# Attention in a macaron block: softmax division by packed rows in place of TensorE transposes

## The chip, the cores and the metric

The kernel runs on one core of a Trainium2 chip. The metric is the device time of one execution in microseconds, as the median of several runs. TensorE multiplies matrices into eight PSUM banks of 128 x 512 f32; VectorE, ScalarE and GpSimd (POOL) work elementwise; SyncE (SP) issues nearly all DMAs, in program order.

## The reference, cut to what matters

```python
def attn(x, Wq, Wk, Wv, Wo):              # x: (16, 256, 256), 16 heads of 16
    q, k, v = split_heads(x @ Wq.T), split_heads(x @ Wk.T), split_heads(x @ Wv.T)
    q, k = rope(q), rope(k)
    scores = einsum('bhqd,bhkd->bhqk', q, k) / 4
    scores = where(causal, scores, -inf)
    out = einsum('bhqk,bhkd->bhqd', softmax(scores), v)
    return merge_heads(out) @ Wo.T

x = x + 0.5 * ffn(layernorm(x))           # 256 -> 1024 -> 256, ternary weights, exact gelu
x = x + attn(layernorm(x))
x = x + 0.5 * ffn(layernorm(x))           # same weights
```

## The kernel before

The program has three stages that share the residual `res` in SBUF: a feed-forward stage over 8 chunks of 512 rows, attention over 16 batches of 256 rows, and the feed-forward stage again (FFN2 here). f32 products are made as sums of products of a high and a low part (fp32r, or three bf16 parts for q and k).

Attention is a software pipeline written out by hand. `periods` steps p from -2 to 16; p = 1 to 10 are a hardware loop of five turns with two periods each. Each period has two steps, h = 0 and 1, of eight heads. Every engine has its own `step(p, h)`, and in period p it works on several batches: the loads of batch p+2, the maxima (scores S, with the queries on partitions) of batch p+1, the transposed scores T, exponentials and products with v (PV) of batch p, Q/K/V and rope of batch p+3, layer norm and its transposes XT of batch p+4, and the output product of batch p-1. `p.has(n)` is true where batch p+n exists.

A step has six units of S and six of T on TensorE, alternating. S goes to a ring of three banks (`s_ring`), from which VectorE takes row maxima (`maxima`, L863). The maxima, negated by rows of minus ones, enter T as three more rows of the contraction, so that T is ready for the exponential (ScalarE, L985, from a ring of two banks). A `fence` (L1060) puts the causal mask and a large negative constant into a bank ahead of the products (L1065), as a matmul of the identity with a mask tile. After the units come, in h = 0, OT(p, 0) and QK, in h = 1 ANT, V, OT(p, 1), XT and WO; then MT (transposes of the split maxima, L1141) and PV (L1121, L1124).

PV writes the heads transposed: `o_bank` holds for two groups of four heads, each at partitions 32 j, sixteen rows of numerators and one row of softmax sums, because `v_pad` has v in columns 0 to 15 and a one in column 16 (zeros up to 31). To divide, ScalarE copies the bank to `o_sb` (`copy_heads`, L977). TensorE transposes it back into `o_bank` in four transposes (`OT`, L1134), so that the sum of a row stands beside its numerators. VectorE takes reciprocals and multiplies (`normed_heads`, L899 and L903) into `att`, and PV of the next half waits for that (`normed`). Once both halves are in, four transposes (`ANT`, L1184) turn `att` once more into `mixed[0]`, ScalarE and VectorE split it into `att_t` (`copy_att` L990, `low_att` L909), and `WO` (L1196) multiplies it with Wo into `mixed[1]`, which `add_output` (L921) adds to the residual. `mixed[0]` is also the bank of Q and of XT, `mixed[1]` that of K and V.

SyncE's step is: `load` of q and k of batch p+2 (waits until T of period p has read those rows); in h = 1 the stores of batch p+3, six DMAs, which wait for POOL's `low`; then `max_rows`, the DMA of the maxima of batch p+1.

At the end (p = 15 and 16) FFN2's first hidden products are put between the units (`hidden_ahead`), and its first y products wait for the last output to be in the residual (`wo_done`).

## Time and profile before

| | us |
|---|---|
| median of 3 runs | 603.77 |
| lowest, highest run | 602.36, 604.93 |
| span of the profiled execution | 600.8 |
| TensorE busy (matmuls) | 567.2, 94% |
| VectorE busy | 458.9, 76% |
| ScalarE busy | 345.2, 57% |
| POOL busy | 229.3, 38% |

The span runs from the first instruction to the last of one profiled execution; what lies around it in a run's own time is not in it, so the 603.77 and the 600.8 are about 3 us apart. The profiled execution has no run time of its own beside its span. A busy share is a mean over all three stages.

### The profile page before, as it was taken

To read this page: it belongs to the slowest core of one execution; us is meant where nothing else is said; L and a number is where in the kernel's file an instruction comes from. 1 tells how busy PE (TensorE), PEld (TensorE's weight loads), DVE (VectorE), ACT (ScalarE), POOL (GpSimd) and SP (SyncE) were. 2 spreads that over 40 slices of the span, in tenths; PEclk is the share of its full clock that TensorE was granted. 3 is DMA by queue.
4 is the path that set the end of the run, shared out by engine and by line. 5 is a ranking of instruction groups with operands and counts; after the bars stand their busy time and mean duration, and the time that the engine had idled before them with its cause. 6 is when DMAs were issued, how large, how long until landed. Compare 5 with 4: busy or idle time off the path is not lost.

```text
span 600.8 us, 17866 instructions
## 1 busy us (share of the span) xinstructions
PE 567.2 (94%) x6596; PEld 496.4 (83%) x6596; DVE 458.9 (76%) x928; ACT 345.2 (57%) x610; POOL 229.3 (38%) x446
## 2 busy tenths in 40 slices
PE   1999999999789999999999999999888999999998
PEld 1789999999668888888888888888665788999997
DVE  5977777779797978879788788877562777777765
ACT  2765454546246666776667766567545655455453
POOL 6383333332665354444544445434141033333310
PEclk9999999999999999999999999999989999999999
DMA  6530000000987567654576546765400011111111
GB/s 221 199 112 6 0 0 0 0 0 1 257 219 207 167 164 208 172 157 146 166 204 177 158 139 175 197 186 159 138 2 3 1 36 35 35 35 35 35 35 36
DMA packets 71190, 63.45 MB, mean 106 GB/s; under 512 B 4178, under 2 KB 64370, under 8 KB 71154
## 3 DMA queue, kind: packets, MB, share of 16 engines
q1 hardware_dynamic: 69970, 62.81, 36.1%
q8 instruction: 25, 0.41, 0.3%
q10 hardware_dynamic: 1184, 0.14, 0.2%
q14 instruction: 11, 0.09, 0.1%
HBM read 33.03 MB, written 29.36 MB: 104 GB/s over the span
## 4 chain that ended last, share of the span: by engine, by line
PE 82%; DVE 10%; DMA 3%; ACT 2%; issue 1%; POOL 1%; SPq 1%; ACTq 0%; DVEq 0%
PE bank L173 18%; PE bank L537 18%; PE bank L1065 13%; PE bank L673 6%; PE bank L1060 6%; PE bank L1121 5%; PE bank L1196 4%; PE bank L1161 3%; PE bank L156 2%; PE bank L1124 2%; PE bank L1134 2%; DVE mx L863 2%; DVE g_lo L257 2%; PE bank L1184 1%; DMA w1f<-w1t 1%
## 5 line engine op out<-in xcount | busy, mean ns | idle before, releaser
L863 DVE TENSOR_REDUCE mx<-bank 128x2 f32<-128x512 f32 (+1 forms) x192 | 118.7, 684 | 31.3 <-PE bank L1065 31.2
L240 ACT ACTIVATE g<-bank,b1c 128x512 f32<-128x512 f32 x128 | 88.0, 690 | 65.6 <-PE bank L173 62.5
L537 PE MATMUL bank<-w2q,g_hi 128*128 128x256 f32 x512 | 124.4, 284 | 1.3 <-DVE g_lo L257 0.9
L537 PE MATMUL bank<-w2q,g_lo 128*128 128x256 f32 x512 | 122.5, 280 | 0.0
L985 ACT ACTIVATE probs<-bank 128x512 f32<-128x512 f32 x192 | 111.2, 597 | 11.9 <-PE bank L1065 4.4
L537 PEld LDWEIGHTS bank<-w2q,g_hi 128*128 128x128 f32 x512 | 96.5, 188 | 2.9 <-DVE w2q L375 1.1
L537 PEld LDWEIGHTS bank<-w2q,g_lo 128*128 128x128 f32 x512 | 96.5, 188 | 0.6
L315 POOL TENSOR_TENSOR res<-res,b2h 128x1024 f32 (+1 forms) x16 | 38.3, 2394 | 133.0 <-DVE xn L147 128.9
L257 DVE TENSOR_TENSOR g_lo<-g,g_hi 128x512 fp32r<-128x512 f32 x128 | 82.8, 689 | 3.1
L173 PE MATMUL bank<-xt_hi,w1q 128*128 128x512 f32 x240 | 77.3, 404 | 2.0 <-DVE xt_lo L167 2.0
L173 PE MATMUL bank<-xt_lo,w1q 128*128 128x512 f32 x240 | 76.4, 400 | 0.0
L1065 PE MATMUL bank<-k,q 99*64 99x128 bf16 (+1 forms) x1024 | 74.4, 246 | 0.0
L1065 PE MATMUL bank<-q,k 102*64 102x256 bf16 (+1 forms) x1024 | 74.3, 246 | 0.0
L173 PEld LDWEIGHTS bank<-xt_lo,w1q 128*128 128x128 f32 x240 | 46.0, 192 | 11.0
L173 PEld LDWEIGHTS bank<-xt_hi,w1q 128*128 128x128 f32 x240 | 44.4, 192 | 12.1 <-issue 3.0
L1060 PE MATMUL bank<-mask_qk,ident_b 128*64 128x128 bf16 (+1 forms) x384 | 47.4, 243 | 4.5 <-DMA k<-qk_slots 1.8
L1060 PE MATMUL bank<-mask_kq,ident_b 128*64 128x128 bf16 (+1 forms) x384 | 48.1, 247 | 1.1 <-ACT probs L985 1.0
L805 POOL TENSOR_TENSOR rot<-by_cos,by_sin 128x512 f32<-128x512 f32 x30 | 38.3, 1280 | 24.1 <-DVE by_sin L683 23.1
L248 DVE CAST g_hi<-g 128x512 fp32r<-128x512 f32 x60 | 25.6, 427 | 28.4 <-ACT g L240 26.9
L162 ACT CAST xt_hi<-bank 128x512 fp32r<-128x512 f32 x32 | 17.3, 590 | 51.3 <-PE bank L156 51.3
L1019 ACT COPY mt<-bank 24x256 bf16<-24x256 bf16 x32 | 11.6, 361 | 58.3 <-PE bank L1141 57.7
L792 POOL TENSOR_TENSOR m_parts<-mx,zero 128x16 bf16<-128x16 f32 x32 | 8.3, 258 | 95.4 <-DVE mx L863 95.4
(129 smaller groups left out, 1170.1 us busy)
## 6 DMA issues: line engine op xcount, KB each, us to landing
qk_slots<-parts SPq DMA_DIRECT2D x32, 384.0 KB, 3.6
q<-qk_slots SPq DMA_DIRECT2D x32, 384.0 KB, 4.0
k<-qk_slots SPq DMA_DIRECT2D x32, 384.0 KB, 4.5
qk_slots<-parts SPq DMA_DIRECT2D x32, 256.0 KB, 3.4
res<-x SPq DMA_DIRECT2D x8, 512.0 KB, 3.6
qk_slots<-parts SPq DMA_DIRECT2D x32, 128.0 KB, 3.2
out<-res SPq DMA_DIRECT2D x7, 512.0 KB, 2.9
w1f<-w1t SPq DMA_DIRECT2D x2, 512.0 KB, 6.1
```

What stands on the lines that cost most here:

```text
L173: last = nc.tensor.matmul(to[:], w1q[:, k, f * P:(f + 1) * P], part[:, k, :], start=i == 0, stop=i == 2 * KC - 1)
L240: nc.scalar.activation(g[:, f, :], of[:], ACT.Gelu, bias=b1c[:, f:f + 1]).then_inc(g_ready, 1)
L257: nc.vector.tensor_tensor(g_lo[:, f, :], g[:, f, :], g_hi[:, f, :].bitcast(F32), ALU.subtract)\
L315: pool.tensor_tensor(res[:, bass.ts(c, CT), :], res[:, bass.ts(c, CT), :], b2h[:].unsqueeze(1).broadcast_to([P, CT, D]), ALU.add).then_inc ...
L537: last = nc.tensor.matmul(to[:, 0:D], part[:, f, t * P:(t + 1) * P], w2q[:, f, :], start=f == 0 and part is g_hi, stop=f == FC - 1 and par ...
L673: last = nc.tensor.matmul(to[:, e * SEQ:(e + 1) * SEQ], w[i][:, k, (2 * t + e) * P:(2 * t + e + 1) * P], x[a][:, k, :], start=n == 0, stop ...
L805: pool.tensor_tensor(rot[:, t, :], by_cos[:, t, :], by_sin[:, t, :], ALU.add).then_inc(rot_s, 1)
L863: nc.vector.tensor_reduce(o, i, AX.X, ALU.max).then_inc(s_done, 1)
L985: nc.scalar.activation(probs[g % 2][:, 512 * u:512 * u + 512], t_ring[n % 2][:], ACT.Exp, scale=0.25)\
L1060: nc.tensor.matmul(to[c, :, c], ident_b[:, c], mask[:, :, c], start=True, stop=False, skip_group_check=True)
L1065: last = nc.tensor.matmul(to[c, :], weights[:, c], moving, start=False, stop=stop, skip_group_check=True)
L1121: nc.tensor.matmul(o[32 * j:32 * j + 32, :], v_pad[par][:, 0, HALF * h + 4 * g + j, :], probs[g][:, j * SEQ:(j + 1) * SEQ], start=True, st ...
```

## The change

The division no longer goes through TensorE. `pad_cols` is all ones, so columns 16 to 31 of `v_pad` all hold ones and the sums stand in rows 16 to 31 of each group. After `copy_heads`, SyncE's new `heads(p, h)` issues five DMAs: one takes the four rows of sums of `o_sb` into `den`, spread over 128 partitions with 16 values each, and four take the numerator rows to their places in `att`, which is now transposed (rows are head and feature, columns are group and query). After both halves VectorE takes one reciprocal of all sums (`reciprocals`). `reciprocal_rows` writes the result to DRAM (`rden_dram`), waits for it and reads it back with every sum repeated for its sixteen rows (`rden_rows`). `normed_heads` is then one product of 128 x 512, from which `copy_att` and `low_att` make `att_t` without a transpose. The rows of Wo are permuted on the host to match. PV waits only for `copy_heads`.

The order is changed with it: `normed_heads` comes first in step h = 1 on VectorE, `low_att` after three of the six maxima, `copy_att` on ScalarE after three of the six exponentials. `hidden_ahead` of chunk part 2 comes later, the output of batch 14 (period 15) is put into period 16, and the output of batch 15 (period 16) into FFN2: its product is taken on VectorE inside chunk 0, its output product is issued on TensorE after chunk 0 into bank 5, and added after chunk 0.

The masks are stored once and repeated by a stride of 0 in `fence`. Some small constants now lie in the memory of `by_cos`; `rope_products` first waits for the constant rows' DMAs.

```diff
@@ -57,6 +57,7 @@
 
 
         scratch = nc.dram_tensor("qk_slots", (BATCH, 2, SLOTS, 2, HD // 2, HEADS, SEQ), BF16, kind="Internal").ap()
+        rden_dram = nc.dram_tensor("rden_slots", (BATCH, 2, 4 * KC * SEQ), F32, kind="Internal").ap()
...
-        mask_qk = sb("mask_qk", [P, 4, P], BF16)
-        mask_kq = sb("mask_kq", [P, 4, P], BF16)
+        mask_qk = sb("mask_qk", [P, P], BF16)
+        mask_kq = sb("mask_kq", [P, P], BF16)
         ones_mean = sb("ones_mean", [P, P])
-        minus_rows = sb("minus_rows", [PARTS, SEQ], BF16)
-        fence_q, fence_k = sb("fence_q", [FENCE, SEQ], BF16), sb("fence_k", [FENCE, SEQ], BF16)
+        att_t = [sb(f"att_t{n}", [P, KC, SEQ], F32R) for n in ("_hi", "_lo")]
...
+        few = by_cos[0:PARTS, 0, :].bitcast(BF16)
+        fence_q, fence_k, minus_rows = (few[:, i * SEQ:(i + 1) * SEQ] for i in range(3))
+        rows_in = [sem(f"att_rows_in{p}") for p in range(2)]
         parts = [sb(f"parts{p}", [P, 2, PARTS, 2 * SEQ], BF16) for p in range(2)]
+        den, rden = (sb(n, [P, 2, KC * SEQ * 4 // P]) for n in ("den", "rden"))
...
+                                            (mask_qk, 0.0), (mask_kq, 0.0), (pad_cols, 1.0),
...
                         dve.wait_ge(xb_ready, gc + 1)
+                        if opening:
+                            of_last.normed_heads(dve)
                         for t in range(CT):
                             if t == 2 and following is not None and not closing:
                                 if before:
                                     split_xt(dve, n, last_hi, last_lo)
                                 else:
                                     split_xt(dve, n)
+                                if opening:
+                                    of_last.low_att(dve)
...
                         chunk(0, 1, 2, BEGUN)
+                        of_last.add_output(dve)
...
                         chunk(0, True, begun=BEGUN)
+                        of_last.copy_att(act)
...
+                            if phase == 1 and into[f] is banks[5]:
+                                pe.wait_ge(wo_done, BATCH + 1)
...
-                            pe.wait_ge(wo_done, BATCH + 1)
+                            pe.wait_ge(wo_done, BATCH)
...
+                        of_last.output(pe)
...
+        def closes(p, n):
+            return p.known and p.p + n == BATCH - 1
+
+        def o_sb(p, n):
+            return by_cos[:, 0, :] if closes(p, n) else o_all[:]
+
+        def att(p, n):
+            return rot[:, 0, :] if closes(p, n) else att_all[:]
+
+        def rden_rows(p, n):
+            return rot[:, 1, :] if closes(p, n) else rden_all[:]
...
+        def normed_heads(dve, p):
+            dve.wait_ge(heads_in, 128 * p.p)
+            dve.wait_ge(rden_in, 16 * p.p)
+            o = att(p, -1)
+            nc.vector.tensor_tensor(o, o, rden_rows(p, -1), ALU.mult).then_inc(normed, 1)
+
+        def copy_att(act, p):
+            act.wait_ge(normed, p.p)
+            nc.scalar.copy(att_t[0][:].rearrange("p k s -> p (k s)"), att(p, -1)).then_inc(att_hi_s, 1)
+
+        def low_att(dve, p):
+            dve.wait_ge(att_hi_s, p.p)
+            nc.vector.tensor_tensor(att_t[1][:].rearrange("p k s -> p (k s)"), att(p, -1),
+                                    att_t[0][:].rearrange("p k s -> p (k s)").bitcast(F32), ALU.subtract).then_inc(att_lo_s, 1)
+
+        def output(pe, p, to=mixed[1]):
+            pe.wait_ge(att_lo_s, p.p)
+            if p.has(3):
+                pe.wait_ge(v_done, p.p + 4)
+            elif p.has(-2):
+                pe.wait_ge(wo_done, p.p)
+            for t in range(QT):
+                for n, (w, a, k) in enumerate(PASSES):
+                    last = nc.tensor.matmul(to[:, t * D:(t + 1) * D], att_t[a][:, k, t * P:(t + 1) * P], wo[w][:, k, :],
+                                            start=n == 0, stop=n == len(PASSES) - 1)
+            last.then_inc(wo_ready, 1)
+
+        def add_output(dve, p, of=mixed[1]):
+            b = p.p - 1
+            dve.wait_ge(wo_ready, b + 1)
+            nc.vector.tensor_tensor(res[:, bass.ts(b, QT), :], of[:].rearrange("p (t d) -> p t d", t=QT),
+                                    res[:, bass.ts(b, QT), :], ALU.add).then_inc(wo_done, 1)
...
+            def heads(p, h):
+                n, half = -1 if h == 0 else 0, (h + 1) % 2
+                sp.wait_ge(o_copied, 2 * p.p + h)
+                if half == 0 and p.has(-1) and not closes(p, n):
+                    sp.wait_ge(att_lo_s, p.p)
+                if half == 0 and p.has(-1) and closes(p, n):
+                    sp.wait_ge(den_s, p.p)
+                of, to = o_sb(p, n), att(p, n)
+                sp.dma_start(den[:, half, :], of[HD:P:32, :]).then_inc(den_in, 16)
+                for j in range(4):
+                    row = (4 * half + j) * HD
+                    sp.dma_start(to[row:row + HD, :], of[32 * j:32 * j + HD, :]).then_inc(heads_in, 16)
+
+            def reciprocal_rows(p):
+                sp.wait_ge(den_s, p.p)
+                sp.dma_start(rden_dram[p.p - 1].rearrange("h (p c) -> p h c", p=P), rden[:]).then_inc(rden_out, 16)
+                sp.wait_ge(rden_out, 16 * p.p)
+                sp.dma_start(rden_rows(p, -1), rden_dram[p.p - 1].rearrange("h (j s) -> h j s", j=4).unsqueeze(2)
+                             .broadcast_to([2, 4, HD, KC * SEQ])).then_inc(rden_in, 16)
+
             def step(p, h):
+                if p.has(-1) if h == 0 else p.has(0):
+                    heads(p, h)
+                if h == 0 and p.has(-1):
+                    reciprocal_rows(p)
                 if p.has(2):
                     load(p, h)
                 if h == 1 and p.has(3):
...
+            def reciprocals(p):
+                dve.wait_ge(den_in, 32 * p.p)
+                nc.vector.reciprocal(rden[:], den[:]).then_inc(den_s, 1)
...
                 opening = p.known and p.p == FIRST
-                if p.has(1):
-                    maxima(p, h)
+                last = p.known and p.p == BATCH
                 if h == 0:
+                    if p.has(1):
+                        maxima(p, 0)
+                    if p.has(-1) and not last:
+                        reciprocals(p)
...
-                    if p.has(-1):
-                        normed_heads(p, 0)
...
+                    if p.has(-1) and not last:
+                        normed_heads(dve, p)
+                    if p.has(1):
+                        maxima(p, 1, range(3))
+                    if p.has(-1) and not last:
+                        low_att(dve, p)
+                    if p.has(1):
+                        maxima(p, 1, range(3, 6))
...
-                    if p.has(-1):
-                        low_att(p)
-                    if p.known and p.p == BATCH:
+                    if last:
                         then.cast_by_dve(dve, CHUNKS, 3)
                         then.low_part(dve, CHUNKS, 2)
                         then.low_part(dve, CHUNKS, 3)
+                        reciprocals(p)
+                        add_output(dve, Period(BATCH - 1))
                     if p.has(3):
                         take_rest(p, 0)
                         take_rest(p, 1)
-                    if p.has(0):
-                        normed_heads(p, 1)
                     if p.has(4, 2):
                         low_xt(p)
-                    if p.has(-1):
-                        add_output(p)
+                    if p.has(-1, 0, BATCH - 3):
+                        add_output(dve, p)
...
             def copy_heads(p, h):
-                j = 2 * p.p + h - 1
-                act.wait_ge(pv_done, j + 1)
-                nc.scalar.copy(o_sb[:].rearrange("p g s -> p (g s)"), o_bank[:]).then_inc(o_copied, 1)
-
-            def exponentials(p, h):
-                for n in range(6 * h, 6 * h + 6):
+                n = -1 if h == 0 else 0
+                act.wait_ge(pv_done, 2 * p.p + h)
+                if p.has(-1):
+                    act.wait_ge(heads_in, 64 * (2 * p.p + h - 1))
+                    act.wait_ge(den_in, 16 * (2 * p.p + h - 1))
+                nc.scalar.copy(o_sb(p, n), o_bank[:]).then_inc(o_copied, 1)
+
+            def exponentials(p, h, units=range(6)):
+                for n in (6 * h + i for i in units):
...
+                last = p.known and p.p == BATCH
+                if last and h == 0:
+                    for f in (2, 3):
+                        then.gelu(act, CHUNKS, f, banks[f])
+                    then.cast_by_act(act, CHUNKS, 2)
                 if p.has(-1) if h == 0 else p.has(0):
                     copy_heads(p, h)
-                if p.has(0):
-                    exponentials(p, h)
+                if h == 0 and p.has(0):
+                    exponentials(p, 0)
                 if h == 1:
-                    if p.has(-1):
-                        copy_att(p)
+                    if p.has(0):
+                        exponentials(p, 1, range(3))
+                    if p.has(-1) and not last:
+                        copy_att(act, p)
+                    if p.has(0):
+                        exponentials(p, 1, range(3, 6))
...
-                    nc.tensor.matmul(to[c, :, c], ident_b[:, c], mask[:, :, c], start=True, stop=False, skip_group_check=True)
+                    nc.tensor.matmul(to[c, :, c], ident_b[:, c], mask[:, c].unsqueeze(1).broadcast_to([P, to.shape[1], HALF_ARRAY]), start=True, stop=False, skip_group_check=True)
...
-                    pe.wait_ge(normed, 2 * p.p + h)
+                    pe.wait_ge(o_copied, 2 * p.p + h)
...
-            def OT(p, h):
-                j = 2 * p.p + h - 1
-                pe.wait_ge(o_copied, j + 1)
-                for t in range(QT):
-                    for g in range(2):
-                        last = nc.tensor.transpose(turn_bank[:, (2 * t + g) * P:(2 * t + g + 1) * P], o_sb[:, g, t * P:(t + 1) * P],
-                                                   ident[:])
-                last.then_inc(turned, 1)
...
-                if p.has(-1):
-                    pe.wait_ge(att_lo_s, p.p)
-                else:
-                    pe.wait_ge(rope_s, 2 * (b - 1) + 1)
+                pe.wait_ge(rope_s, 2 * (b - 1) + 1)
...
-                    if p.has(-1):
-                        OT(p, 0)
...
-                    if p.has(-1):
-                        ANT(p)
                     if p.has(3):
                         V(p)
-                    if p.has(0):
-                        OT(p, 1)
                     if p.has(4, 2):
                         XT(p)
+                    if closing:
+                        pe.wait_ge(mt_sb, 2 * BATCH)
+                        hidden_ahead(pe, 2)
                     if last:
                         hidden_ahead(pe, 5)
                         hidden_ahead(pe, 6)
-                    if p.has(-1):
-                        WO(p)
+                        output(pe, Period(BATCH - 1))
+                    if p.has(-1, 0, BATCH - 3):
+                        output(pe, p)
...
+        end = Period(BATCH)
+        return Stage(sync, gpsimd, vector, scalar, tensor, LastOutput(
+            lambda dve: normed_heads(dve, end), lambda act: copy_att(act, end), lambda dve: low_att(dve, end),
+            lambda pe: output(pe, end, o_bank), lambda dve: add_output(dve, end, o_bank)))
...
-        "wo": inputs["L0_attn_Wo"].T,
+        "wo": inputs["L0_attn_Wo"].T.reshape(2, 2, 4, HD, D).transpose(1, 0, 2, 3, 4).reshape(D, D),
```

## Rows read from the trace of the kernel before

**Rows 1.** The page, chain that ended last: share of the span by engine.

```profile
PE 82%; DVE 10%; DMA 3%; ACT 2%; issue 1%; POOL 1%; SPq 1%; ACTq 0%; DVEq 0%
```

**Rows 2.** Windows: us, busy PE, PEld, DVE, ACT, POOL, clock, DMA share, GB/s.

```profile
241.80:260.60 18.80, 18.68 (x314) 16.26 (x309) 16.26 (x34) 12.65 (x24) 9.66 (x21) 1.00 0.60 169
```

**Rows 3.** Chain in order of time, one period: start us, us, what.

```profile
248.64 0.23 PE bank L1060 x2
...
252.42 0.59 PE bank L1134 x4
...
257.44 0.23 PE bank L1060 x2
...
261.22 0.59 PE bank L1184 x4
...
263.22 0.44 PE bank L1134 x4
...
267.26 0.23 PE bank L1060 x2
```

**Rows 4.** Timeline of SyncE's queue, same period: start us, us, what.

```profile
247.53 4.57 SPq L689 DMA_DIRECT2D qk_slots<-parts  x6
...
252.20 0.76 SPq L759 DMA_DIRECT2D q<-mt  x1
...
261.93 0.32 SPq L747 DMA_DIRECT2D k<-qk_slots  x1
```

**Rows 5.** Timeline of VectorE, same period: start us, us, what [idle before].

```profile
249.25 3.68 DVE L863 TENSOR_REDUCE mx<-bank 128x4 f32<-128x512 f32 x6 [1.32 <-PE bank L1065]
...
252.84 0.73 DVE L876 TENSOR_SCALAR xn<-res,mean,rstd 128x256 f32 x2
...
253.49 0.26 DVE L899 RECIPROCAL rden<-bank 128x16 f32<-128x16 f32 x1
...
253.77 0.42 DVE L903 TENSOR_TENSOR att<-bank,rden 128x256 f32<-128x256 f32 x1
...
254.47 0.69 DVE L680 TENSOR_TENSOR by_cos<-bank,cos_t 128x512 f32<-128x512 f32 x1 [0.28 <-PE bank L673]
...
256.52 0.75 DVE L683 TENSOR_TENSOR by_sin<-bank,sin_t 128x256 f32<-128x256 f32 x2
...
258.05 1.29 DVE L863 TENSOR_REDUCE mx<-bank 128x4 f32<-128x512 f32 x2 [0.79 <-PE bank L1065]
```

**Rows 6.** Landing by line: L299 (output, 128 KB), L689 (stores), L747 (loads).

```profile
DMA to landing us min/median/max: 1.7/1.8/3.8
...
DMA to landing us min/median/max: 2.4/3.4/5.2
...
DMA to landing us min/median/max: 3.1/4.1/6.1
```

**Rows 7.** Chain in order of time, periods 12 to 14.

```profile
410.96 0.60 ACT probs L985
...
412.03 1.14 ACT parts L997 x2
...
417.03 0.23 PE bank L1060 x2
...
421.39 0.23 POOL m_parts L792
...
422.55 0.29 PE bank L1141 x2
...
433.36 0.23 PE bank L1060 x2
```

**Rows 8.** Busy time by windows, the end of attention.

```profile
433.40:476.60 43.20, 37.44 (x501) 28.92 (x501) 22.59 (x48) 26.78 (x47) 9.47 (x26) 0.96 0.01 3
...
438.00:440.00 2.00, 0.37 (x3) 0.14 (x3) 1.82 (x6) 0.49 (x2) 1.44 (x7) 1.00 0.00 0
...
440.00:444.00 4.00, 4.00 (x58) 3.01 (x60) 1.86 (x5) 1.03 (x2) 1.82 (x5) 0.59 0.03 7
```

More of the change, by code:

```diff
@@ L379, in turn_first @@
                     def turn_first():
+                        for rows in rows_in:
+                            dve.wait_ge(rows, 48)
                         for t in range(2):
@@ L603, in _ @@
             attend.vector(dve, after.helpers)
-            after.vector(dve)
+            after.vector(dve, attend.helpers)
         @block.scalar
@@ L665 @@
 Stage = namedtuple("Stage", "sync gpsimd vector scalar tensor helpers")
+LastOutput = namedtuple("LastOutput", "normed_heads copy_att low_att output add_output")
 Turning = namedtuple("Turning", "scratch by_cos by_sin rot rest parts qk_ready rope_s rot_s top_s rest_s mid_s low_s stored")
@@ L1046, in step @@
                     then.cast_by_act(act, CHUNKS, 0)
-                if p.known and p.p == BATCH and h == 0:
-                    for f in (2, 3):
-                        then.gelu(act, CHUNKS, f, banks[f])
-                    then.cast_by_act(act, CHUNKS, 2)
             act.preload_act_table(ACT.Exp)
```

113 lines of the change are left out of this document (30 added, 83 removed).

## The prediction

> **What bounds the kernel now.** I read the chain that ended last first [rows 1]: TensorE makes up 82% of it. A stretch of one period of the attention loop [rows 2] shows what that means: of 18.8 us TensorE is busy for 18.7 and VectorE for 16.3. So the loop is bound by TensorE, with VectorE 2.5 us behind it.
>
> Then I read the chain in order of time through one period p [rows 3] and counted from its start at 248.64. Step h=0 runs 8.80 us: scores and transposed scores until +3.78, the OT transposes (L1134, 0.59 us), Q/K, MT, PV. Step h=1 begins at +8.80 (257.44). Its scores end at +12.58 (261.22); then ANT 0.59, V, OT 0.44, XT, WO, MT, PV until 267.26. From the scores' end to the next period are 6.04 us.
>
> Last I read what the two engines that get new work do in that period. The SyncE queue [rows 4] is full over its start: six stores of the period before issue from 247.53 for 4.57 us, then the row maxima's DMA, so the queue is free at 252.96, **+4.32**. VectorE [rows 5] goes from its h=0 maxima to xn at +4.2 (252.84), does rope from +5.83 to +8.63 (254.47 to 257.27) and begins the h=1 maxima at +9.41, 0.6 us after TensorE begins that step.
>
> **What the change removes.** Twelve transposes per period leave TensorE: 0.59 + 0.59 + 0.44 = **1.62 us** of the chain [rows 3]. Taken alone, the period would be 18.8 - 1.6 = 17.2. VectorE loses two reciprocals (0.26) and two products (0.42) and gets one reciprocal (0.26) and one product of 512 columns (0.69, as by_cos): 1.36 against 0.95, so its work does not bind. ScalarE keeps the same copies; the cast of att moves from after the scores into their middle. The stride-0 mask gives TensorE as many columns as the copies did, so I price it at nothing, though nothing would hide it; no row has such an operand on TensorE, and on VectorE the broadcast cosines of by_cos cost no more than a plain product (0.69 for 512 columns, 0.42 for 256 [rows 5]); bounds 0 and 0.1 us a period. The constants' shorter selects lie in the first microseconds of the run beside the weight loads; nothing.
>
> **What it adds: a round trip through SyncE.** In h=0 of period p the queue issues den, four copies of numerator rows, waits for the reciprocals, writes them to DRAM, waits for the landing, and reads them back spread over the rows. It stands in the program after the stores and the maxima's DMA of h=1 of p-1, so it begins no sooner than +4.32, though PV of the half before has ended at the period's start and o_sb follows it.
>
> First VectorE. reciprocals(p) comes straight after the h=0 maxima, at +4.2, but den can only be issued at +4.35. No row shows a small copy from SBUF to SBUF landing. The nearest are 1.8 us for 128 KB of output, 2.4 the least of a store, and 3.1 the least of a load of 384 KB [rows 6]. An output less its bytes (128 KB at the 169 GB/s of [rows 2] are 0.8, at a burst's higher rate less) leaves 1.0 to 1.3. I take 1.8 (bounds 1.0 and 2.4). So den is there at +6.15 and VectorE, which would be idle only 0.3 us, waits 2 us. Behind it stand xn and rope: 0.26 + 0.73 + 2.80 (rope's length in [rows 5]) bring it to **+9.95** (bounds 9.15 and 10.55). Rope's readers can wait (POOL's sums, then ScalarE's casts after the scores), but VectorE enters h=1 at +9.95, not at +8.8, whatever the inverses do.
>
> Then the queue. Five issues: a load's issue takes 0.32, a store's 4.57 / 6 = 0.76, the maxima's SBUF to SBUF one 0.76 [rows 4]. The new ones are of that last kind, so 5 x 0.75 = 3.75 (bounds 1.6 and 4.0). The write of 16 KB goes out at +8.1 and lands 1.8 later (bounds 1.0 and 2.4), +9.9. The read moves 256 KB, between 1.8 for 128 KB and 3.1 for 384 KB: 2.5. With 0.1 for the two wake-ups the inverses are there at **+12.5**, bounds 8.9 and 14.0.
>
> The Trainium skill (DMA: Bandwidth & Descriptors, Anatomy of one DMA) gives each DMA a fixed cost of about 2.0 us, fitted on the GpSimd path, most of it the receipt of the last write. The rows agree in size (1.8 for the output of 128 KB). [...]
>
> **What waits for it.** normed_heads is now ahead of the h=1 maxima on VectorE. TensorE has three banks for the scores: it starts h=1 at +8.2, fills units 6 to 8 and stands before unit 9 until the first maximum is taken. VectorE needs 0.69 for the product, and its maxima go at 3.68 / 6 = 0.61 each [rows 5]; unit 11 needs three of them, then unit 11 and its transposed partner take 3.78 / 6 = 0.63. So the scores end 0.69 + 1.84 + 0.63 = 3.16 us after the inverses land. low_att stands behind those three maxima and costs TensorE nothing. From the scores' end ScalarE sets the pace, as it does in the period of [rows 7]: the last exponential, (now no att cast), two casts, v, then WO, MT, PV; 417.03 - 410.96 = 6.07 there, less the 0.47 from the exponential's end to the casts at 412.03, makes 5.6. Period = landing + 3.16 + 5.6 = landing + 8.8. **The break-even landing is +10.0.** VectorE's own +9.95 already uses all of it; at +12.5 the period is 21.3, **+2.5 us**. Bounds: 18.0 (-0.8, by VectorE's earliest +9.15) and 22.8 (+4.0).
>
> The numerator copies of h=1, the loads and the stores keep slack: the h=1 heads issue at the scores' end for 3.75 us, the two loads after them are needed a period later, the stores are due where they were, about 1.1 us before the next period [rows 4]. The queue then comes free at +4.3 again, so the delay does not grow from period to period.
>
> **How often.** p=1 to 12 each pay 2.5: 30.0. In p=13 the stores of p=12 are still ahead, but there is no Q/K to fill the time. Before it takes 433.36 - 417.03 = 16.3 [rows 7]; after it the maxima's end (landing + 0.69 + 1.84 + 0.69 + 1.84), 1.2 for POOL's split (421.39 to 422.55 [rows 7]) and 1.57 for MT and PV, from the same landing, give 20.3: +4.0. Without stores ahead (p=14, 15) the trip starts at +1 and costs little.
>
> **The end.** From 433.4 to 476.6 TensorE stands idle 43.2 - 37.4 = 5.8 us, and its granted clock is 0.59 on the mean of 440 to 444, after the wait of 438 to 440, which costs 0.41 x 4 = 1.7 us [rows 8]. The wait for normed before PV, the late WO of batch 14 and the last output go; twelve to fourteen transposes go too (about 4 us). All of it would be 11.5 us. But p=14 and 15 have round trips of their own (about 9 us after their start, with h=1 beginning at 5 to 7), and the last products, casts and add are moved into VectorE's queue of FFN2's first chunk, where g_lo is already what TensorE waits for. I take 5 (bounds 0 and 11.5).
>
> **Sum.** 30.0 + 4.0 - 5 - 0.4 (one OT of p=0) = +28.6, taken as +28. The profiled execution's span is 600.8, the median of the runs 603.8; the 3 us lie outside the chain and are kept. 603.8 + 28 = **632 us**.
>
> **Rivals.**
> A. The trip is short: issues at the loads' 0.32 and both landings near 1.8 us, so that the inverses come by +10.0 and VectorE's own +9.95 decides. Then the loop stays at 18.8, p=13 is about even, and the end gives 8: **596 us**, faster. It decides from a landing under +10.4 on. For it: DMA engines are idle after the loads of h=0, the transfers are small. Against: the one SBUF to SBUF issue shown takes 0.76, and with five of those even the least landings (1.0 and 1.8) end at +11.0. Chance 0.13.
> B. About the same: landing at +10.5, 12 x 0.5 = 6 against the end's 7. Chance 0.05.
> C. The clock falls as well. After the idle of 438 to 440 the granted clock fell to the lower level (1.2 GHz) and lost 1.7 us of the 4 that followed [rows 8]. At a landing at +12.5 TensorE stands still for some 3 us in each period. At half clock unit pairs take 1.26 in place of 0.63, slower than VectorE's 0.61; 1.7 x 13 = 22 us at most: **654 us**. For it: the one like wait of before had this effect; against: here exponentials and transposed scores break it. Chance 0.25.
> D. The change does what it says, the trip fully hidden: 16 x 1.62 + 7.5 less: 603.8 - 33 = **571 us**. It needs den in hand at +4.2, before the queue can issue it. Chance 0.02.
> My forecast, slower by the trip with the clock kept: 0.55.
>
> **Numbers.** The chance of faster is A and D, 0.15; within 0.5% (3 us, about what runs of this kernel can tell) 0.05; slower 0.80. The range goes from A's 596 to C's 654 and above it for late landings (+4.0 a period gives 603.8 + 48 + 5 - 5 = 652, the clock on top): 596 to 664. The forecast's own range is 608 to 652.
>
> **What would show it.** In the profile after: a period of about 21.3 us; VectorE idle before the reciprocal until den lands (2 us), and before the 512-column product until the inverses land (2 us or more), both released by DMAs; idle TensorE before the mask matmuls of unit 9, released by maxima; the first den issue of a period right behind the DMA of the maxima. Wrong would be: the queue reaching the den issue before +4, landings of 1.0 us, or a period at or below 18.8.

## The result, and the profile after

The changed kernel took 692.0 us (691.1 to 694.0) where the kernel before took 603.7 in the same measurement: ratio 1.148, 95% interval 1.145 to 1.150. I had predicted 632 us and a range up to 664. The direction was right, the size was not: 88 us more where I had forecast 28. The span of the profiled execution is 690.6 us against 600.8, 89.8 us more.

The page, chain that ended last, shares by engine and then by line (to be read beside [rows 1]):

```profile
PE 47%; SPq 17%; DMA 16%; DVE 8%; issue 4%; ACT 4%; POOL 3%; DVEq 0%; ACTq 0%
```

TensorE's 82% has become 47%, and 33% are now SyncE's issues (SPq) and DMA landings: the loop is no longer bound by TensorE. A landing is the time from a DMA's issue until whoever waits for its data may go on, and a time with a plus sign is counted from the start of its period. Here are one period of the loop (us, busy PE, PEld, DVE, ACT, POOL, clock, DMA share, GB/s), to be read beside [rows 2], and the 4 us after the long wait in it:

```profile
294.90:319.60 24.70, 19.36 (x302) 16.46 (x298) 16.13 (x31) 12.50 (x23) 7.51 (x15) 0.93 0.57 152
310.50:314.50 4.00, 4.00 (x48) 3.55 (x49) 3.91 (x8) 1.65 (x3) 0.12 (x1) 0.60 0.15 35
```

The same period, which starts at 294.91, on SyncE's queue, to be read beside [rows 4]:

```profile
293.60 4.91 SPq L704 DMA_DIRECT2D qk_slots<-parts  x6
298.61 0.83 SPq L815 DMA_DIRECT2D q<-mt  x1
299.86 0.65 SPq L825 DMA_DIRECT2D den<-o_sb  x1
300.56 2.45 SPq L828 DMA_DIRECT2D att<-o_sb  x4
303.21 0.43 SPq L832 DMA_DIRECT2D rden_slots<-rden  x1
304.82 0.73 SPq L834 DMA_DIRECT2D rden_rows<-rden_slots  x1
305.94 0.36 SPq L803 DMA_DIRECT2D q<-qk_slots  x1
```

Here den is issued at +4.95, the write at +8.30, the read at +9.91. On VectorE, beside [rows 5]:

```profile
301.80 0.35 DVE L976 RECIPROCAL rden<-den 128x32 f32<-128x32 f32 x1 [2.52 <-DMA den<-o_sb]
...
309.15 0.69 DVE L765 TENSOR_TENSOR att<-att,rden_rows 128x512 f32<-128x512 f32 x1 [3.76 <-DMA rden_rows<-rden_slots]
309.76 1.88 DVE L943 TENSOR_REDUCE mx<-bank 128x4 f32<-128x512 f32 x3
```

Both waits of the forecast are there: 2.52 us for the sums and 3.76 us for the inverses, which are in hand at 309.13, +14.2. TensorE stands behind the maxima that stand behind the product:

```profile
310.50 0.42 PE L1131 MATMUL bank<-mask_qk,ident_b 128*64 128x256 bf16 x2 [4.33 <-DVE mx L943]
```

It then runs at the lower level of its clock (1.2 GHz): the mean granted clock of the next 4 us is 0.60, and the scores end at 313.93. The next period begins at 319.58. So the period is 14.2 + 4.8 + 5.65 = 24.7 us, where the forecast was 12.5 + 3.16 + 5.6 = 21.3.

From the list of the whole run's waits (engine, line, what it waited for: us in total, times, longest):

```profile
PE bank L1131 <- DVE mx L943: 62.3, 16, 5.8
DVE att L765 <- DMA rden_rows<-rden_slots: 60.8, 15, 7.2
...
DVE rden L976 <- DMA den<-o_sb: 34.1, 14, 4.6
...
ACT o_sb L1047 <- DMA att<-o_sb: 27.0, 13, 5.0
```

The last of these I had not foreseen: ScalarE can't copy the next half's sums into o_sb until the numerator copies have left it. From the starts of the periods in both traces: p=1 to 12 take 303.4 us in place of 224.5 (+78.9, 6.6 each), p=13 22.2 in place of 16.3 (+5.8), and what follows p=13 172.1 in place of 167.5 (+4.6); +0.5 lies ahead of p=1.

### The profile page after: what moved, and what is told of

It is laid out like the page before. It is cut to its first block, busy times and chain, and to the rows that moved or that the text cites. A ratio compares the mean times of both kernels' runs of the same rounds, so it can differ in the third digit from the quotient of the medians.

```text
span 690.6 us, 17763 instructions
## 1 busy us (share of the span) xinstructions
PE 582.6 (84%) x6404; PEld 504.1 (73%) x6404; DVE 456.2 (66%) x896; ACT 344.4 (50%) x610; POOL 226.8 (33%) x445
## 4 chain that ended last, share of the span: by engine, by line
PE 47%; SPq 17%; DMA 16%; DVE 8%; issue 4%; ACT 4%; POOL 3%; DVEq 0%; ACTq 0%
PE bank L550 16%; PE bank L176 15%; DMA rden_rows<-rden_slots 9%; SPq L704 9%; PE bank L1136 6%; SPq L828 5%; DMA rden_slots<-rden 4%; PE bank L1223 3%; PE bank L1131 3%; DVE mx L943 3%; POOL parts L890 2%; PE bank L159 2%; SPq L815 2%; SPq L825 1%; ACT parts L1068 1%
## 5 line engine op out<-in xcount | busy, mean ns | idle before, releaser
L943 DVE TENSOR_REDUCE mx<-bank 128x2 f32<-128x512 f32 (+1 forms) x192 | 120.4, 684 | 19.8 <-PE bank L1136 18.8
L550 PE MATMUL bank<-w2q,g_hi 128*128 128x256 f32 x512 | 125.8, 286 | 3.9 <-DVE res L433 2.7
L1131 PE MATMUL bank<-mask_qk,ident_b 128*64 128x128 bf16 (+1 forms) x384 | 51.6, 264 | 65.6 <-DVE mx L943 62.3
L317 POOL TENSOR_TENSOR res<-res,b2h 128x1024 f32 (+1 forms) x16 | 38.3, 2394 | 138.8 <-DVE xn L150 134.4
L1136 PE MATMUL bank<-k,q 99*64 99x128 bf16 (+1 forms) x1024 | 83.9, 270 | 0.0
L1136 PE MATMUL bank<-q,k 102*64 102x256 bf16 (+1 forms) x1024 | 83.7, 270 | 0.0
L1131 PEld LDWEIGHTS bank<-mask_qk,ident_b 128*64 128x64 bf16 x384 | 23.5, 118 | 76.8 <-DVE mx L943 66.2
L1131 PE MATMUL bank<-mask_kq,ident_b 128*64 128x128 bf16 (+1 forms) x384 | 52.0, 267 | 12.0 <-ACT probs L1055 11.9
L1136 PEld LDWEIGHTS bank<-q,k 102*64 102x64 bf16 x1024 | 49.7, 124 | 1.3
L765 DVE TENSOR_TENSOR att<-att,rden_rows 128x512 f32<-128x512 f32 x15 | 10.4, 693 | 60.8 <-DMA rden_rows<-rden_slots 60.8
```

The costliest lines, as they stand in the source:

```text
L317: pool.tensor_tensor(res[:, bass.ts(c, CT), :], res[:, bass.ts(c, CT), :], b2h[:].unsqueeze(1).broadcast_to([P, CT, D]), ALU.add).then_inc ...
L550: last = nc.tensor.matmul(to[:, 0:D], part[:, f, t * P:(t + 1) * P], w2q[:, f, :], start=f == 0 and part is g_hi, stop=f == FC - 1 and par ...
L943: nc.vector.tensor_reduce(o, i, AX.X, ALU.max).then_inc(s_done, 1)
L1131: nc.tensor.matmul(to[c, :, c], ident_b[:, c], mask[:, c].unsqueeze(1).broadcast_to([P, to.shape[1], HALF_ARRAY]), start=True, stop=False, ...
L1136: last = nc.tensor.matmul(to[c, :], weights[:, c], moving, start=False, stop=stop, skip_group_check=True)
```

## The experiments

Ratios are to the kernel before; "us" is the median. Experiments 1 to 4 were measured beside one set of runs of the kernel before, 5 to 7 beside a second, 8 to 10 beside a third, and 11 and 12 beside a fourth.

**1. The trip left out.** No write and no read of the inverses; VectorE multiplies by a tile of ones, so the output isn't divided.

```diff
 def normed_heads(dve, p):
     dve.wait_ge(heads_in, 128 * p.p)
-    dve.wait_ge(rden_in, 16 * p.p)
...
 def reciprocal_rows(p):
+    return
```

> The changed kernel without the write of the reciprocals to DRAM and the read back (the product is taken with ones instead; the five copies per half, the reciprocals and all other work stay). Theory 'the round trip is the wait': VectorE enters step h=1 right after rope, about 10.5 us after the period's start instead of 14.2; the scores end 3.2 later, the next period starts 5.6 after that, so a period takes about 19.3 us in place of 24.7 and the run about 622 us. Rival 'the copies alone, or the queue's issue work, set the period': it stays above 22 us and the run above 660 us.

Measured: 625.6 us, ratio 1.038 (1.035 to 1.041). The trip holds 66 of the 88 us. The time is near the 622 that I expected, and in part by luck: the periods p=1 to 12 take 20.7 us on average (alternately about 19 and 22) where the theory had 19.3, and the stretch behind p=13 is 9.6 us shorter than in the changed kernel, which the theory didn't count. What is left are the waits for the packing: VectorE waits 42.3 us for den, ScalarE 36.3 us before it may copy into o_sb.

**2. TensorE kept busy through the wait.** Thirty matmuls whose result nobody reads, between units 8 and 9 of the scores, where TensorE waits.

```diff
+if n == 8 and p.has(3) and p.has(-1):
+    pe.wait_ge(rope_s, 2 * (p.p + 3) + 2)
+    for _ in range(30):
+        nc.tensor.matmul(mixed[1][:, 0:D], xt_hi[:, 0, 0:P], wv[0][:, 0, :], start=True, stop=True)
```

> The changed kernel with 30 matmuls of 128x128 by 256 columns, whose result nobody reads, put into TensorE's wait of each period (before unit 9 of the scores), so that TensorE is busy for 3.6 us of it. Theory 'the half clock after the wait is a large part': the granted clock stays at full, the scores end 3.2 us after the inverses land instead of 4.8, 13 periods are 1.6 shorter: about 671 us. Rival 'the clock costs nothing, VectorE sets the pace after the landing': 690 us or more.

Measured: 684.9 us, 1.138 (1.133 to 1.144); mean granted clock 0.975 against 0.931. In the period below the filling runs from 305.88 to 309.67 and unit 9 starts at 309.91, still behind VectorE's first maximum, so the filling itself costs nothing. The clock is kept in more than half of the periods (seven of the thirteen have no stretch at the lower level, where the changed kernel has none such), and only 6 to 7 us come back: nearer to the rival's 690 than to the theory's 671. The chain in order of time over one period says why (start us, us, what):

```profile
304.62 3.91 DMA rden_rows<-rden_slots
309.17 0.82 DVE mx L943 x2
...
313.36 1.39 DVE stats L947 x4
314.75 0.60 DVE rest L972
315.38 0.63 ACT parts L1068
316.07 1.18 POOL parts L890
317.41 0.42 SPq L704
...
323.76 0.64 SPq L825
...
326.32 1.96 DMA att<-o_sb
```

This is a closed cycle that TensorE is hardly in. The inverses land, VectorE takes its six maxima and (in every second period) the statistics of x, and only then come the rest of the turned q and k, its casts, and their six stores (317.41, whose issues fill SyncE until 322.8). Den, the numerators, the write and the next read stand behind those stores: the next read is issued at 328.73, **24.1 us** after this one at 304.62. Over the reads of p=1 to 13 the distance is 24.4 us on average here and 25.0 in the changed kernel, and twelve times this difference is about the 7 us. The lower clock hardly enters the cycle: from the landing to the end of VectorE's sixth maximum are 4.9 us here and 5.1 in the changed kernel. With the full clock TensorE does begin its next period earlier (it starts at 317.5, 9.0 us after the landing, where the forecast had 8.8 and the changed kernel takes 10.45), but the queue comes free later in that period, den is issued at +6.3 and not +4.95, and most of the gain is given back.

**3. The trip ahead of the stores of K.** SyncE's order alone is changed: stores of Q, sums and numerators, maxima's DMA, write, read, then the stores of K.

```diff
 def step(p, h):
     if p.has(-1) if h == 0 else p.has(0):
         heads(p, h)
+    if h == 0 and p.has(0) and not (p.known and p.p == FIRST):
+        max_rows(p, 1, -1)
     if h == 0 and p.has(-1):
         reciprocal_rows(p)
+    if h == 0 and p.has(2) and not (p.known and p.p == FIRST):
+        store_turned(sp, turning, p.p + 2, p.parity(2), 1, K_RUNS)
...
-        store(p, 1, K_RUNS)
```

> The changed kernel with SyncE's queue in another order alone: the copies of h=0, the maxima's DMA and the round trip are issued ahead of the three stores of K of the batch. Theory 'the place in the queue makes the trip late': den goes out about 1.3 us after the period's start in place of 4.95, the write at about 5.2, the read at 6.8, the landing at 9.3 to 11; a period is 18.2 to 20 us, the run 600 to 625 us. Rival 'the latencies of the three DMAs in line are the cost, wherever they start': the period stays above 23 us, the run above 670 us.

Measured: 649.4 us, 1.076 (1.071 to 1.081), between the two. The order is worth 43 us, and the wait for the inverses falls to 45.1 us. The stores of Q are still ahead: in the period that starts at 300.33 den goes out at +2.0 and not at +1.3, and the read at +8.3 (+7.4 on average of p=1 to 12) and not at +6.8. The distance from one read to the next is 21.8 us on average, 3.2 less than in the changed kernel: the stores of K have left the cycle.

**4. The product later, nothing else.** In the order of the changed kernel VectorE multiplies after all six maxima and the two rests.

```diff
 if p.has(1):
-    normed_heads(dve, p)
-    maxima(p, 1, range(3))
-    low_att(dve, p)
-    maxima(p, 1, range(3, 6))
+    maxima(p, 1)
 ...
+normed_heads(dve, p)
+low_att(dve, p)
```

> The changed kernel with the product by the inverses, the cast and the subtraction put after the six maxima of h=1 (on VectorE) and after the exponentials and the copy of v (on ScalarE); SyncE's order is as it was. Theory 'the wait costs because the scores stand behind it': TensorE no longer waits at unit 9, the wait moves to the output product; but the copies of h=1 wait for the subtraction, and behind them the loads and stores, so SyncE's cycle of about 21.5 us becomes the bound: about 650 us. Rival 'place of use doesn't matter, the queue's chain sets the period anyway': within 10 us of 692.

Measured: 696.1 us, 1.156 (1.152 to 1.160). The rival was right, and the theory's cycle of 21.5 us was too short: the periods p=1 to 12 take 25.6 us on average. TensorE waits for the maxima for 3.2 us in place of 62.3, and nothing is won:

```profile
ACT o_sb L1044 <- DMA att<-o_sb: 66.8, 19, 5.4
...
DVE rden L976 <- DMA den<-o_sb: 61.7, 14, 5.5
...
PEld bank L1127 <- ACT probs L1052: 45.7, 30, 4.0
...
PE bank L784 <- DVE att_t_lo L773: 33.8, 14, 3.5
...
PE bank L1127 <- DVE mx L943: 3.2, 5, 1.5
```

SyncE copies the numerators of h=1 into att only when the low part of the batch before is made. That is now late, and the loads and stores stand behind it in its order.

**5. The masks alone,** on the kernel before.

```diff
-mask_qk = sb("mask_qk", [P, 4, P], BF16)
+mask_qk = sb("mask_qk", [P, P], BF16)
...
+mask[:, c].unsqueeze(1).broadcast_to([P, to.shape[1], HALF_ARRAY])
```

> The kernel before, with one part of the change alone: the causal masks kept once (128x128) and read with a zero stride by the mask matmuls and the fills of the constants. Theory: a moving operand with a zero stride costs TensorE nothing, and the trace of the changed kernel shows no slower mask matmul; expected the same as before within 0.5% (603 us). Rival: a zero stride reads slower; at 0.1 us for each of the mask matmuls' groups (6 a period, 16 periods) the time would be 612 us.

Measured: 602.9 us, 0.9986 (0.9970 to 1.0002). The stride-0 operand costs nothing that these runs can tell.

**6. The read alone in the queue.** SyncE issues the two loads behind the read only when it has landed.

```diff
 reciprocal_rows(p)
+sp.wait_ge(rden_in, 16 * p.p)
```

> The changed kernel with one wait more: SyncE issues the two loads behind the read of the inverses only when the read has landed. In the changed kernel the landing took 4.31 us from the read's issue, and packets of the loads, issued 1.1 and 1.7 us behind it, were mixed among its own. Theory one (loads mixed in delay the read): the landing falls to about 2.8 us, VectorE starts the product 1.5 us earlier in each of 13 periods, and the time falls by about 18 us to 674 us. Theory two (the read's own 1024 rows of 2048 bytes take that long, or it waits for the write's tail): the landing stays at about 4.3 us and the time stays within 5 us of 692 us, or rises, as the loads come 3 us later.

Measured: 682.8 us, 1.129 (1.125 to 1.133): 9 us less than the change by the medians, 11 by the ratios, between the two theories. SyncE and then VectorE in it, in the period of above:

```profile
304.89 0.73 SPq L834 DMA_DIRECT2D rden_rows<-rden_slots  x1
```

```profile
308.60 0.69 DVE L765 TENSOR_TENSOR att<-att,rden_rows 128x512 f32<-128x512 f32 x1 [3.15 <-DMA rden_rows<-rden_slots]
```

3.7 us, against 4.3. Over p=1 to 12 the averages, from the read's issue to the product, are 3.9 and 4.3. So the loads delay the read by 0.4 to 0.6 us of the 1.8 by which my forecast missed it; the other 1.2 to 1.4 stay with the read alone. (The read writes 128 rows of 2048 bytes, not the 1024 of the expectation.)

**7. The rearrangement.** Two o_sb and two att buffers (the second ones in parts of v_all that are spent by then), each half with its own semaphores; the order of experiment 3, but with the read behind the stores of K; the product after the six maxima, the cast and the low part later still; the output product of a pair one period later, ahead of Q/K.

```diff
+spent = v_all[:].rearrange("p t d -> p (t d)")
-o_all = sb("o_sb", [P, KC * SEQ])
+o_all = [sb("o_sb0", [P, KC * SEQ])[:], spent[:, KC * SEQ:2 * KC * SEQ]]
...
-    maxima(p, 1, range(3))
+    maxima(p, 1)
...
+    normed_heads(dve, p)
...
+if p.has(-2, 0, BATCH - 3):
+    output(pe, p, later=1)
```

> The changed kernel rearranged around the same packing and the same round trip: two buffers for the sums and numerators (o_sb) and two for the packed rows (att), the second ones in a part of v_all that is spent by then, so that no copy of a head waits for the landing of the one before; SyncE issues the packing of h=0, the transposed maxima and the write of the inverses ahead of the stores of K, and the read behind them; VectorE multiplies by the inverses after the six maxima of h=1 and makes the low part later still; the output product of a pair comes one period later, ahead of the scores. Theory (the change lost its time to the wait for the trip and to the half clock that follows, not to the work of the trip itself): TensorE is the bound again, without the twelve transposes that the change removed, at 17.2 to 18 us a period and full clock: 575 to 600 us. Rival: SyncE's own instructions of a period (about 17.7 us of issues and the 1.6 us until the write has landed) or the trip's latency still bound it: 19.5 us a period or more, 612 us or more.

Measured: 614.5 us, 1.019 (1.014 to 1.024). 77 of the 88 us are back with the same packing and the same trip. But the time is the rival's (612 or more), and the period lies between the theory's 18 and the rival's 19.5: 19.0 us in the middle of the loop, 19.2 on average over p=1 to 12. In every period VectorE still waits for the sums, 0.4 to 3.1 us, ahead of adding the output product:

```profile
314.12 0.35 DVE L991 RECIPROCAL rden<-den 128x32 f32<-128x32 f32 x1 [1.77 <-DMA den<-o_sb]
```

**8. The reciprocals behind that addition,** and FFN2's closing product behind two of its four results.

```diff
-if p.has(-1) and not last:
-    reciprocals(p)
...
 add_output(dve, p, later=1)
...
+if p.has(-1) and not last:
+    reciprocals(p)
```

> The rearranged kernel (x8_combo), in which VectorE waited 1.8 to 2.8 us for the sums ahead of adding the output product, and TensorE stood still behind it (0.83 us in every second period, 4.34 us in the last but one). Edits: the reciprocals come after the output product is added, and in FFN2 the closing product of numerators and inverses comes after two of the four results. Theory (those waits are what is left): about 0.4 us in each of 13 periods, 3 to 4 us in the last but one and 2 us in FFN2: 604 us, from 614.5. Rival: SyncE is the bound and the waits only move (write and read of the inverses come later, the product waits for them): within 3 us of 614.5 us.

Measured: 611.6 us, 1.012 (1.010 to 1.014): 3 to 4 us less, under half of what I expected and, by the medians, still within the rival's 3 us. VectorE's wait for the sums is all but gone (17.9 us in experiment 7, 1.3 here), so it was hardly what held that kernel up.

**9. The read left out of that kernel** (the output isn't divided).

```diff
 def read_rows(p):
     sp.wait_ge(rden_out, 16 * p.p)
+    sp.sem_inc(spare, 1)
+    return
```

> x9_sums_late with the read of the inverses left out (the write stays, VectorE multiplies by ones, so the output is not divided). Theory (in the rearranged kernel the trip is hidden, and the time is set by TensorE's own work and its small gaps): at most 3 us below x9_sums_late. Rival (the read's 256 KB and its landing still cost): 6 us or more below it.

Measured: 604.7 us, 1.002 (1.001 to 1.004), 6 to 7 us less: the rival. Even a trip that the steady periods cover costs some 6 us in all. In p=5 to 10 both kernels take 18.6 us a period; the difference lies in the periods before and behind, and why it lies there was not tried.

**10. The product put back ahead of the maxima,** in the kernel of experiment 8.

```diff
+normed_heads(dve, p)
 maxima(p, 1)
-normed_heads(dve, p)
```

> x9_sums_late with one order put back: VectorE multiplies by the inverses ahead of the six maxima of h=1, nearly where the changed kernel has it. Theory (where the wait for the trip stands on VectorE is what decides, whatever the buffers and the queue's order are): the product waits about 4 us a period ahead of maxima that TensorE waits for, and the clock falls to half behind it: 650 us or more. Rival (two buffers and the earlier issue of the trip are enough): within 8 us of x9_sums_late.

Measured: 671.2 us, 1.111 (1.106 to 1.117). One instruction's place in VectorE's order makes **60 us**. First VectorE, then TensorE in it:

```profile
304.56 0.69 DVE L769 TENSOR_TENSOR att<-att,rden_rows 128x512 f32<-128x512 f32 x1 [4.70 <-DMA rden_rows<-rden_slots]
305.17 3.84 DVE L957 TENSOR_REDUCE mx<-bank 128x4 f32<-128x512 f32 x6
```

```profile
305.91 0.30 PE L1146 MATMUL bank<-mask_qk,ident_b 128*64 128x256 bf16 x2 [3.92 <-DVE mx L957]
```

In the kernel of experiment 8 the same two lines stand in the other order, and the product waits for nothing:

```profile
301.96 3.68 DVE L957 TENSOR_REDUCE mx<-bank 128x4 f32<-128x512 f32 x6 [0.69 <-PE bank L1151]
305.71 0.69 DVE L769 TENSOR_TENSOR v_all<-v_all,rden_rows 128x512 f32<-128x512 f32 x1
```

**11 and 12. What the missing transposes leave open.** Kernel 11 is that of experiment 8 with VectorE's statistics of x moved behind the rests, and its last xn between the maxima. Kernel 12 besides puts P·V ahead of the transposes of the maxima, since TensorE in experiment 8 waits there for GpSimd:

```profile
308.41 0.29 PE L1218 MATMUL bank<-ident_b,m_parts 128*128 128x128 bf16 x2 [1.22 <-POOL m_parts L892]
```

```diff
+if p.has(0):
+    PV(p, h)
 if p.has(1):
     MT(p, h)
-if p.has(0):
-    PV(p, h)
```

> x9_sums_late with VectorE's statistics of x moved behind the rests of the turned q and k (ScalarE's copies and the next scores wait for the rests), and, in the last but one period, its normalised x behind three of the six maxima of h=1. Theory (TensorE's stops of 0.5 to 1.3 us, and the half clock behind the longer ones, come from VectorE's order): 0.4 us in each of 13 periods, two windows of half clock early in the stage (3.4 us together) and 3 us in the last but one period: 600 us. Rival (the stops move to the next late step): within 3 us of x9_sums_late (610 to 611.5 us).

> x12_stats_late with TensorE's products of probabilities and v ahead of the transposes of the maxima, which wait 1.2 us in every second period for GpSimd's four operations; before the change the twelve transposes of the heads lay in that place and covered the wait. Theory: the 1.2 us are covered again, 0.6 us a period on average, 5 to 8 us below x12_stats_late. Rival (the maxima's copy then holds the bank that the next scores need, and the stop only moves there): within 3 us of x12_stats_late, or above it.

Measured: kernel 11 takes 609.5 us, 1.012 (1.010 to 1.015), no gain that can be told from experiment 8; kernel 12 takes 606.9 us, 1.006 (1.005 to 1.008), less by 2.6 us (medians) or 3.4 (ratios), nearer the rival than the theory. Five periods of before, and then five of kernel 12, by windows:

```profile
276.10:369.60 93.50, 93.15 (x1542) 81.29 (x1542) 79.05 (x157) 62.89 (x115) 43.74 (x90) 1.00 0.59 170
```

```profile
281.20:371.20 90.00, 88.16 (x1482) 75.08 (x1480) 79.05 (x147) 59.55 (x116) 50.69 (x90) 1.00 0.77 205
```

Here the change does at last what it can: 60 fewer matmul records and 5.0 us less TensorE work in five periods, and the period is 18.0 us in place of 18.7. It is still no faster than before as a whole. The other periods of the loop give that gain back (p=2 to 5 take 19.0 to 20.5 us each), so that p=1 to 12 take 223.8 us against 224.5; p=13 takes 1.7 us more than before, and what follows it 3.9. At the start of p=14 TensorE waits for the loads:

```profile
434.63 0.43 PE L1148 MATMUL bank<-mask_qk,ident_b 128*64 128x256 bf16 x2 [3.64 <-DMA k<-qk_slots]
```

No version of the changed kernel beats the kernel before.

## Why the prediction was wrong, point by point

The mechanism that I forecast is there: VectorE waits for the sums, then for the inverses, and TensorE waits for the maxima behind them. Three steps failed. The read's landing was mis-sized (2.5 us, measured 4.3), the clock was taken to be kept (it fell in every period; in the one read above it put off the scores' end by 1.6 us), and the delay was taken to be counted from TensorE's start, where stores, sums, write and read close a cycle of their own (periods of 25.3 us, forecast 21.3).

**TensorE's saving was over-sized.** "1.62 us of the chain" added up three rows of [rows 3]. The windows of experiment 12 measure 5.0 / 5 = 1.0 us a period: those rows hold the time for which each group of transposes stood on the chain, and I take the rest to be time that the following matmuls need in any case, which no run here separates. Nor does the 1.0 us shorten the kernel by itself. Five periods of experiment 8:

```profile
282.80:375.90 93.10, 87.99 (x1482) 74.84 (x1480) 79.25 (x147) 60.99 (x115) 48.25 (x90) 1.00 0.72 196
```

TensorE is busy for 88.0 of 93.1 us, and the period is 18.6 us as before. The wait of 1.22 us for GpSimd in every second period stands behind the place where the transposes had been, and with P·V ahead of it (kernel 12 against kernel 11) 3 us came back.

**The queue: nearly right.** Forecast, then measured: den issued +4.35, +4.95; sums in hand +6.15, +6.9; write +8.1, +8.3; write landed and read issued +9.9, +9.91. The five issues took 3.15 in place of 3.75 (den 0.65, four of 0.61), which made good the later start. The write's landing, 1.59, was within its bounds. VectorE was through with rope at +10.5, forecast +9.95 and 10.55 at most.

**The read's landing: the first step that failed.** "The read moves 256 KB ... 2.5" was 4.3. The term was mis-sized: it lay between the median of an output of 128 KB (1.8) and the least of the loads of 384 KB (3.1), while the same rows have medians of 4.1 for the loads and 3.4 for the stores [rows 6]. Experiment 6 gives 0.4 to 0.6 of the 1.8 to the loads issued right behind the read, which the forecast didn't count. The rest is there without them: in each of the changed kernel's 16 trips the read's first packet starts 1.4 to 1.5 us after the issue began, and in the loop the last one ends 3.2 to 3.5 us after it. The Trainium skill (DMA: Bandwidth & Descriptors, Anatomy of one DMA) gives a fixed cost of about 2.0 us per DMA besides its bytes; an estimate by it, from the write's issue at +8.1, is 2.0 for the write, 2.0 + 0.6 for the read and 0.1 for the wake-ups, so +12.8. That is nearer than my +12.5, but the measured +14.2 is above both: the write landed in 1.6, less than by the Trainium skill's figure, and the read in 4.3, more than its 2.6.

**The clock: the second step that failed.** I priced rival C at 1.7 us a period (0.41 x 4 is 1.64), and that was its size: the scores ended 4.8 us after the landing and not 3.16. What was wrong was its chance, 0.25, against a forecast "with the clock kept". The rows that I had shown had such a fall already, after a stretch in which TensorE was busy for 0.37 of 2 us [rows 8]; here the wait is longer (4.33 us in the row above), and each of the thirteen periods from p=1 to 13 has a stretch at the lower level.

**The sum of those two** is 1.7 + 1.6 = 3.3 us a period: 21.3 becomes 24.7 (the last 0.1 us is rounding), and 12 x 3.3 = 40 us of the 60 by which the forecast fell short. That adds up one period as it stands. It doesn't say that either term, mended alone, gives its share back: with the clock mostly kept (experiment 2) 7 us came back and not 1.6 x 12 = 19.

**"The delay does not grow from period to period": the step behind both.** I held the stores to be due where they were, 1.1 us before the next period, and counted each period from TensorE's start. But maxima, rests, casts, stores, sums, write and read are one closed cycle through VectorE and SyncE, 24.1 us long in the period shown of experiment 2, and TensorE only follows it. That is why the full clock returned little, why a later product alone returned nothing (experiment 4), and why the order of the queue alone returned 43 us (experiment 3). The cycle itself is read off one period of experiment 2; that it bounds the changed kernel too is my reading of experiments 2 to 4 together. The mean period is 25.3 and not 24.7: 6.6 us over before, 12 times.

**The end: wrong in sign.** Forecast -5, measured +4.6 behind p=13. Without the trip (experiment 1) the same stretch is 5.0 us shorter than before, what I had foreseen. With it, p=14 takes 19.2 us as before (17.7 in experiment 1), in p=15 VectorE waits 5.5 us for a read of its own, and then, in FFN2's first chunk:

```profile
567.16 2.08 DVE L765 TENSOR_TENSOR rot<-rot 128x512 f32<-128x512 f32 x1 [1.03 <-DMA rot<-rden_slots]
```

VectorE holds up FFN2's results for a product that stands ahead of them. It waits 1.0 us for the read, and the product takes 2.08 us where the others of its size take 0.69; an operation of GpSimd (L317, 128x1024) runs beside it from 566.34 to 568.69. Whether that is the cause was not tried. p=13 was forecast at +4.0 and measured +5.8.

**The masks** cost nothing, as priced (experiment 5).

In sum, the 89.8 us between the spans are 30 + 4 - 5 - 0.4 as forecast, 40 for the landing and the clock, 9 for periods that are longer still (12 x 6.6 = 79 against 30 + 40), 2 for p=13, 10 for the end, and 1 ahead of p=1.

## What to carry to other kernels

When a round trip through memory is put into a software pipeline, draw the whole cycle that it closes, with the queue's other DMAs in it, and add that up before any engine's own period. A wait priced at one place says little if the cycle runs elsewhere. An instruction that waits for a landing belongs behind everything on its engine that another engine waits for: here that place was worth 60 us (experiment 10), but only together with second buffers and another order of the queue; alone it was worth nothing (experiment 4). And instructions taken off the bounding engine count only for what they keep it busy, less the waits that they were covering.

## What the runs showed of the hardware

- A DMA from SBUF to SBUF of 32 KB (16 partitions to 16 others) landed 1.9 to 3.1 us after its issue in the changed kernel, median 2.0, and an issue took 0.59 us. A write of 16 KB to DRAM landed in 1.6 us (median; 3.1 at most). A read of the same 16 KB that writes 256 KB, each sum sixteen times, was in VectorE's hands 3.6 to 4.2 us after its issue when nothing was issued behind it (experiment 6, p=1 to 12), and 3.8 to 4.6 with two loads of 384 KB issued 1.1 and 1.7 us behind it.
- GpSimd's four small operations on the maxima (128 x 16) mostly took 0.22 to 0.32 us each in experiment 8, but the four from 305.80 on took 0.54 to 0.69, beside VectorE's product and rests. They stand on the way to TensorE, which waited 1.2 us for them there. In the changed kernel a product of VectorE took 2.08 us in place of 0.69 beside a large operation of GpSimd (at 567.16). What the two engines share there wasn't tried.
- In the changed kernel TensorE's granted clock fell to the lower level (1.2 GHz) in each of the thirteen periods p=1 to 13, in the row above after a wait of 4.33 us. In experiment 8 it stayed at the upper level through gaps of 1.2 us from 259 to 406 us of the run. In experiment 2 matmuls whose result nobody reads, put into the wait, kept it at the upper level through seven of the thirteen periods.
